# Third layer's weight product as seven half-size products over pairs of tiles, in a fused four-layer graph network

## The reference, cut to what matters

```python
h = jnp.maximum(_layernorm(x, axis=-1), 0.0)
# _L2_gnn_ref: self loops are added to the edges first
norm = dinv[src] * dinv[dst]
h = h @ W                                  # W is 1024 x 1024
out = jax.ops.segment_sum(h[src] * norm[:, None], dst, num_segments=n) + b
x = x + jax.nn.relu(out)
h = jnp.maximum(_layernorm(x, axis=-1), 0.0)   # and the fourth layer: h @ W, attention
```

## Time and profile before

| | |
|---|---|
| time, median of three runs | 986.05 us |
| span of the profiled execution | 985.7 us |
| TensorE busy with matmuls | 968.1 us, 98% |
| VectorE, ScalarE, GpSimd busy | 664.2, 468.8, 138.7 us |
| the third layer's weight product, first matmul to the first of the next layer | 613.70 to 723.40 us |
| in that stage: VectorE, ScalarE busy | 38.5, 12.9 us |

### The profile page before, as it was taken

The page is one execution under the profiler, slowest core; times in us unless marked ns, Lnnn a source line. Parts: engine busy times, 40 slices in busy tenths (PEclk is TensorE's granted clock), DMA queues, the critical chain, the costliest instruction groups (busy, mean ns, idle before and its releaser), DMA issues.

```text
span 985.7 us, 14150 instructions
## 1 busy us (share of the span) xinstructions
PE 968.1 (98%) x5199; PEld 805.6 (82%) x5200; DVE 664.2 (67%) x1193; ACT 468.8 (48%) x719; POOL 138.7 (14%) x191
## 2 busy tenths in 40 slices
PE   4999999999999999999999999999999999999998
PEld 3888878888888888888888888888888888888887
DVE  6987798788788779378884115333346664967777
ACT  5778864554554547223335446001012232766654
POOL 3022400000000001223331000010000000333331
PEclk9999999999999999999999999999999999999999
DMA  6256490000000005543422040733232130201222
GB/s 237 104 191 228 129 268 1 1 23 0 0 21 0 0 0 118 103 147 125 141 93 65 1 172 8 280 118 107 86 128 70 69 122 1 86 20 66 85 85 81
DMA packets 26006, 88.29 MB, mean 90 GB/s; under 512 B 3384, under 2 KB 3580, under 8 KB 25808
## 3 DMA queue, kind: packets, MB, share of 16 engines
q1 hardware_dynamic: 15072, 52.82, 14.8%
q0 software_dynamic: 10880, 34.74, 11.6%
HBM read 59.23 MB, written 33.56 MB: 94 GB/s over the span
## 4 chain that ended last, share of the span: by engine, by line
PE 95%; DVE 1%; ACT 1%; POOL 1%; DMA 1%; issue 0%; SPq 0%; ACTq 0%; DVEq 0%; POOLq 0%
PE ps L615 22%; PE ps L2271 13%; PE ps L2245 11%; PE ps L2165 9%; PE ps L2166 9%; PE ps L2167 9%; PE ps L2221 5%; PE ps L2217 5%; PE ps L598 3%; PE ps L2088 2%; PE ps L2090 1%; PE ps L2089 1%; PE ps L2013 1%; PE ps L2016 1%; PE ps L2057 1%; PE ps L2282 1%
## 5 line engine op out<-in xcount | busy, mean ns | idle before, releaser
L2165 PE MATMUL ps<-g_hi,mask_hi 128*128 128x512 f32 x400 | 157.7, 394 | 0.2 <-DVE mask_lo L1628 0.2
L2167 PE MATMUL ps<-g_hi,mask_lo 128*128 128x512 f32 x400 | 155.9, 390 | 0.0
L2166 PE MATMUL ps<-g_lo,mask_hi 128*128 128x512 f32 x400 | 155.8, 389 | 0.0
L1144 ACT ACTIVATE mask<-ps,v 128x640 f32<-128x640 f32 x80 | 63.2, 793 | 95.7 <-PE ps L2167 49.1
L2271 PE MATMUL ps<-y_all,att_hi 128*128 128x512 f32 x380 | 103.6, 392 | 0.0
L2165 PEld LDWEIGHTS ps<-g_hi,mask_hi 128*128 128x128 f32 x400 | 75.1, 188 | 19.0 <-DVE mask_lo L1628 2.3
L581 ACT ACTIVATE hT_hi<-ps 128x1024 fp32r<-128x1024 f32 x30 | 30.8, 1026 | 123.6 <-PE ps L598 123.4
L2167 PEld LDWEIGHTS ps<-g_hi,mask_lo 128*128 128x128 f32 x400 | 75.1, 188 | 16.0
L2166 PEld LDWEIGHTS ps<-g_lo,mask_hi 128*128 128x128 f32 x400 | 75.1, 188 | 14.8
L615 PE MATMUL ps<-w,hT_hi 128*128 128x512 f32 x320 | 86.6, 392 | 0.0
L2271 PEld LDWEIGHTS ps<-y_all,att_hi 128*128 128x128 f32 x380 | 70.4, 188 | 14.8 <-issue 0.4
(11 more groups left out here) (232 smaller groups left out, 1968.3 us busy)
## 6 DMA issues: line engine op xcount, KB each, us to landing
xin<-x_after SPq DMA_DIRECT2D x20, 512.0 KB, 3.2
xres<-x_after POOLq DMA_DIRECT2D x20, 512.0 KB, 3.6
x_after<-xres POOLq DMA_DIRECT2D x20, 512.0 KB, 2.9
w_raw<-in_L_gnn_W SPq DMA_DIRECT2D x8, 1024.0 KB, 9.8
x_after<-g POOLq DMA_DIRECT2D x20, 256.0 KB, 7.6
xin<-in_x SPq DMA_DIRECT2D x9, 512.0 KB, 3.5
x_after<-in_x SPq DMA_DIRECT2D x8, 512.0 KB, 5.2
weight_rows<-weight_row POOLq DMA_DIRECT2D x8, 512.0 KB, 3.8
```

The lines of the kernel that those rows point to most:

```text
L1144: nc.scalar.activation(mask[k][:, :], U_ALL, ACT.Tanh, bias=v[:, s:s + 1]).then_inc(tanh_ready, 1)
L2165: nc.tensor.matmul(SUMS[dd], mask_hi[k][:, cols], g_hi[:, s, :], start=(s == 0), stop=False)
L2166: nc.tensor.matmul(SUMS[dd], mask_hi[k][:, cols], g_lo[:, s, :], start=False, stop=False)
L2167: last = nc.tensor.matmul(SUMS[dd], mask_lo[k][:, cols], g_hi[:, s, :], start=False, stop=(s == T - 1))
```

## The change

Two tiles of neighbour sums, t and t + 5, are taken as the rows of a 2x2 block matrix (A11, A12 above A21, A22, each 128 rows by 512), the weight as another (B11, B12, B21, B22, each 512 x 512). Their product of eight half-size block products is replaced by one of seven (Winograd's form). For each of the five pairs there are seven **units**, each of 4 blocks by 3 products, 12 matmuls of 128x512 into one bank. The left sides are A11, A12, A22 and four sums S1 to S4 (S1 = A21 + A22, S2 = S1 - A11, S3 = A11 - A21, S4 = A12 - S2), the right sides B11, B21, B22 and four sums T1 to T4. The stream's order is the list `UNITS`.

What this brings with it:

- The factor `dis` of a row is now multiplied in while a pass's banks are read (`take_pass`, one VectorE instruction instead of ScalarE's copy and VectorE's subtraction). For that `dis` is written to DRAM and read back as a row on all partitions.
- VectorE adds and subtracts the blocks S1 to S4 (`add_block`, 20 instructions of 128x512) and the weights' sums (`w2_sum`, 8 of 128x1024).
- Each unit's left side gets its high part from ScalarE (`part_hi_of`) and its low part from VectorE (`part_lo_of`), 35 of each, three units ahead. The seven right sides are split in 14 pieces of 128x1024 on either engine, ten of them during the units (`SPLIT_AT`).
- Each unit's bank is read by one VectorE instruction that adds it to the running sum (`take_unit`, 35 of 128x512). Twenty of these are final halves of a tile; ScalarE takes their positive part (`relu_of`), and GpSimd adds them in DRAM to the layer's input with an accumulating DMA (20 of 256 KB, `add_unit`), in place of ten loads, L1829 and ten stores.
- The third layer's weight is loaded before the passes and not in them; the fourth layer's in two halves behind units 19 and 24. Its eight splits stand at units 25 to 34 (`W3_AT`), the statistics of the fourth layer's first tiles at 28 and 29. The transposes stand in the middle of the last unit.

A unit waits for its left side's low part, its right side's, and for the bank's former user (`unit_read`). The core of the diff:

```diff
+UNITS = ([("A11", t, B11) for t in range(PAIRS)] + [("A12", t, B21) for t in range(PAIRS)] + [("S2", t, T2) for t in range(PAIRS)]
+         + [("S1", t, T1) for t in range(PAIRS)] + [("S4", t, B22) for t in range(PAIRS)]
+         + [unit for n in range(PAIRS + 1) for unit in ([("S3", n, T3)] if n < PAIRS else []) + ([("A22", n - 1, T4)] if n > 0 else [])])
+UNIT_BANKS = (0, 1, 6, 7, 0, 1, 6, 7, 0, 1, 2, 3, 4, 5, 2, 3, 4, 5, 2, 3, 0, 1, 4, 5, 0)
+LATE_BANKS = (1, 2, 3, 0, 1)
+BANK_OF = [LATE_BANKS[t] if kind in ("S3", "A22") else UNIT_BANKS[n] for n, (kind, t, _) in enumerate(UNITS)]
+SPLIT_AT = {0: (T2, 0), 1: (T2, 1), 3: (T1, 0), 4: (T1, 1), 6: (B22, 0), 7: (B22, 1), 11: (T3, 0), 12: (T3, 1), 16: (T4, 0), 17: (T4, 1)}
+W3_AT = {25: 0, 26: 1, 27: 2, 28: 3, 30: 4, 31: 5, 33: 6, 34: 7}
...
+        for n in range(len(UNITS) + 1):
+            if n + BLOCK_LEAD < len(UNITS):
+                part_hi_of(n + BLOCK_LEAD)
+            if n in SPLIT_AT:
+                w2_hi_of(*SPLIT_AT[n])
+            if n - 1 in RELU_UNITS:
+                relu_of(n - 1)
+            if n in W3_AT:
+                split3_act(W3_AT[n])
+            if n in (len(UNITS) - 4, len(UNITS) - 3):
+                h_act(act, dense[2], 0, n - (len(UNITS) - 4))
+            if n == len(UNITS) - 1:
+                transposed_act(act, dense[2], 0, 0)
+                root_act(act, dense[2], 0)
```

```diff
+        for n in range(len(UNITS) + 1):
+            if n + BLOCK_LEAD < len(UNITS):
+                part_lo_of(n + BLOCK_LEAD)
...
+            if n > 0:
+                take_unit(n - 1)
+            if 1 <= n <= PAIRS:
+                add_block("S1", n - 1)
+                add_block("S2", n - 1)
+            if 1 <= n - PAIRS <= PAIRS:
+                add_block("S4", n - PAIRS - 1)
+            if 13 <= n < 13 + PAIRS:
+                add_block("S3", n - 13)
+            if n in SPLIT_AT:
+                w2_lo_of(*SPLIT_AT[n])
+            if n in W3_AT:
+                split_dve(dve, dense[2], [W3_AT[n]])
+            if n in (28, 29):
+                stats_dve(dve, dense[2], 0, n - 28)
+            if n == 29:
+                variance_dve(dve, dense[2], 0)
+            if n == len(UNITS) - 1:
...
+                transposed_dve(dve, dense[2], 0, 0)
...
+        def unit_pe(n):
+            kind, t, w = UNITS[n]
+            pe.wait_ge(part_lo_ready, n + 1)
+            pe.wait_ge(w2_lo_ready, 2 * w + 2)
+            users = [m for m in range(n) if BANK_OF[m] == BANK_OF[n]]
+            if users:
+                pe.wait_ge(unit_read, users[-1] + 1)
...
+            for k in range(QK):
+                if k == QK // 2 and n == len(UNITS) - 1:
+                    transpose_pe(pe, dense[2], 0, 0)
+                for left, rights in ((of[:, 0, k, :], (W2_HI[w], W2_LO[w])), (of[:, 1, k, :], (W2_HI[w],))):
+                    for right in rights:
+                        last = nc.tensor.matmul(UNIT_BANK[n], left, right[:, k, :],
```

More of the change, by code:

```diff
@@ L787, in _ @@
         load_x3(1)
-        sp.wait_ge(w_lo_ready, KT * 4)
-        with sp.Fori(2, HT) as i:
+        sp.wait_ge(w_lo_ready, KT * 3)
+        for i in range(2, HT):
             load_x3(i)
@@ L1248, in _, with relu_of, split3_act @@
+        def relu_of(n):
+            act.wait_ge(unit_read, n + 1)
+            nc.scalar.activation(unit_sum(n), unit_sum(n), ACT.Relu).then_inc(relu_done, 1)
+        def split3_act(k):
+            blocks, adds, pieces = W3_FREE[k]
+            act.wait_ge(part_lo_ready, blocks)
+            act.wait_ge(add_done, adds)
+            act.wait_ge(w2_lo_ready, pieces)
+            split_act(act, dense[2], [k])
         for t in range(T):
@@ L1265, in _ @@
                 root_act(act, d, (t + 2) // 2)
-        last_pass = T * (len(PASSES) - 1)
+        early = {T * FIRST_HALF + n: piece for n, piece in enumerate(((B11, 0), (B11, 1), (B21, 0), (B21, 1)))}
         for n in range(T * len(PASSES)):
@@ L1791, in _ @@
         hs_lo_of(T - 1)
-        d2 = dense[2]
         def low_counts(p):
@@ new lines, in w2_sum, with part_lo_of @@
+        def w2_sum(to, left_of, right_of, op):
+            for j in range(2):
+                some = slice(2 * j, 2 * j + 2)
+                nc.vector.tensor_tensor(to[:, some, :], left_of[:, some, :], right_of[:, some, :], op).then_inc(w2_chain, 1)
+        def part_lo_of(n):
+            kind, t, _ = UNITS[n]
+            of = parts[n % BLOCK_RING]
+            dve.wait_ge(part_hi_ready, n + 1)
+            nc.vector.tensor_tensor(of[:, 1, :, :], sums_block(kind, t), of[:, 0, :, :].bitcast(F32), ALU.subtract).then_inc(part_lo_ready, 1)
@@ L1831, in _ @@
[L1831 to L1845 removed]
+            if p == 0:
+                dve.wait_ge(consts_landed, 48)
@@ L1847, in scores @@
+        scale_dve(dve, dense[2], 0)
+        d3 = dense[2]
         def scores(i, b):
@@ L2251, in _ @@
-        for t in range(T):
-            gcn_product(t)
+        def unit_pe(n):
[5 more added lines that the diff above has]
+                pe.wait_ge(unit_read, users[-1] + 1)
+            elif BANK_OF[n] in (2, 3, 4, 5):
+                pe.wait_ge(sums_read, 2 * len(PASSES))
+            else:
+                pe.wait_ge(sums_read, 2 * len(PASSES) - 2)
+            of = parts[n % BLOCK_RING]
+            for k in range(QK):
[4 more added lines that the diff above has]
+                        last = nc.tensor.matmul(UNIT_BANK[n], left, right[:, k, :],
+                                                start=(kind != "A22" and k == 0 and len(rights) == 2 and right is W2_HI[w]),
+                                                stop=(k == QK - 1 and len(rights) == 1), skip_group_check=True)
+            last.then_inc(unit_done, 1)
@@ L2255, in spread_al @@
+        for n in range(len(UNITS)):
+            unit_pe(n)
         def spread_al(tiles):
```

405 lines of the change are left out of this document (257 added, 148 removed).

## The result

The changed kernel takes 988.88 us, the median of seven runs (986.06 to 991.1), against 986.05 us for the kernel before (also a median of seven). The ratio is 1.0029, with a 95% interval from 1.0018 to 1.0041: slower by 0.3%. The prediction had 985.05 us and "within 0.2%" as the likeliest; its range ended at 988.6, just short of the result.

A forecast was written before the change was run, and what follows sets the result against it. TensorE's matmuls were taken to bound the kernel. The stage going from 109.7 to 107.0 us saves 2.7, a clock fall costs 1.7: 986.05 - 2.7 + 1.7 = 985.05 us, range 982.6 to 988.6.

The forecast's parts named there:

- What the change takes away: In the changed stage 60 matmuls of 0.2267 us fall away, 13.6 us; the new stage takes at least 96.1 us.
- The passes keep their matmuls: In the passes ahead of the stage, the matmuls stay as they were; no cost was put on it.
- The first units: Stage start to unit 11: VectorE's work ends at 27.8 us, before unit 11 starts at 29.9; costed at nothing.
- The room of 2 us: VectorE's spare time up to unit 11's low part, 2.1 us, or 0.055 us per instruction.
- The last ten units: End of stage: VectorE and ScalarE wait for each other, rounds of 4.1 us against 2.72 per unit; 10.9 us of stalls.
- The clock: Behind the 4.9 us stall before the fourth layer's product the clock likelier falls than not; price 0 to 2.3, taken 1.7 us.
- the circle: Late units: ScalarE's weight copy waits behind its positive part, that for VectorE's taking, VectorE's low part for the copy; 4.1 us.
- What was costed at nothing: DMA landings, one-instruction pass reading, weight sums in the fourth pass and GpSimd's additions: 0; a failed landing 0 to 3 us.
- That the clock holds: Rival for the stall before the fourth layer: no clock fall, 983.35 us, between 982.6 and 984.1; chance 0.22.
- That VectorE's instructions are dearer: Rival for the stage: each VectorE instruction 0.06 to 0.18 us more, taken 0.12, giving 990.65 us; chance 0.20.
- That the splits hide: Rival for the last units: no mutual waiting, only a 1.3 us tail from the transposed tile, 973.75 us; chance 0.04.
- That a landing is late: Rival: a DMA behind units 9, 24 or 28 adds 1 to 3 us, giving 986 to 988; chance 0.12.

The follow-up runs named there:

- the filled kernel: Changed kernel with extra matmuls into unread banks ahead of units 31, 33, 34 and behind the last unit, where TensorE would stand: 986.24 us.
- the doubled sums: Changed kernel with 15 more VectorE additions of the same size behind block sums of the first ten units: 993.14 us.
- the kernel with four moves: Changed kernel with weight copies before positive parts, three third-layer weight loads later, transposes with their splits earlier, shifts at units 29 and 32: 973.68 us, stage 97.70.

## Why the prediction was wrong, by its steps

- **What the change takes away**, 13.6 us and a floor of 96.1 for the stage: right. The best kernel comes to 97.70.
- **The step that failed** is "The passes keep their matmuls". They do, 480 of them, but the prediction took from it that they keep their time. It had the loads of the third layer's weight ahead of the passes in its list of what the change brings, where in truth they are issued inside the first one, and gave them no price. It did not ask what of TensorE's stream passes by while they are in flight. There is a branch, and the two together cost 2.7 to 3.2 us in the median: 1.4 to 1.75 of stall, and a clock fall worth 1.8, in two executions of three by the mean clocks of the filled kernel. Without it the kernel takes 985.07 or 985.62 us, by the way it is taken out; the prediction was 985.05.
- **The first units** cost nothing: right. VectorE's low part of unit 11 ends at 641.72 in the changed kernel (its row is at 641.03, 0.69 long), 28.0 us after the stage began, predicted 27.8. The room of 2 us is confirmed by the doubled sums. That VectorE catches up behind unit 12 is right only in the end. It takes unit 17 at 666.75, some 4 us behind that unit's last matmul (613.75 + 18 x 2.72 = 662.7), and TensorE does not wait, as that bank is next written by unit 23. From unit 20 to 24 another round between the two engines stands in the trace, which the prediction had not written down:

```profile
673.26 0.69 DVE L1966 TENSOR_TENSOR parts<-sums,parts 128x512 fp32r<-128x512 f32 x1 [1.22 <-ACT parts L1362]
673.87 0.68 DVE L2007 TENSOR_TENSOR top_right<-ps,second_sum 128x512 f32<-128x512 f32 x1
```

  VectorE waits 1.22 us for the left side's high part, which stands behind the positive part on ScalarE, and the takings at 671.37 and 673.87 are 2.50 us apart, just under a unit's 2.72.
- **The last ten units**: right, in the mechanism (the copy moved by one statement takes 7.7 us out of the stage), in the round (4.08 for 4.1), in the place of each stall and in the length (106.62 for 107.0). The 108.7 us in its paragraph on the profile after is a slip: it adds the clock's 1.7, which by its own account come behind the stage.
- **The clock** behind the stall of 4.5 us: right that it falls, and the size of 1.7 was somewhat low. One execution lost 1.56, another 2.8, outside of the bound of 2.3; the median loses 2.1 to 2.3, by the runs with the stalls filled. So some 0.5 us of the miss are this term's. Right too that a fall in the shorter stalls of the circle costs nothing.
- **What was costed at nothing**: the landings of DMAs, the weights' sums and GpSimd's additions cost nothing, as said. But GpSimd's additions do not all fall where VectorE is ahead: from 663 to 671 us they stretch the instructions of a VectorE that is behind (see the end).
- **The rivals.** That the clock holds gave 983.35; a kernel in which it does, and without the branch, took 983.28. That VectorE's instructions are dearer is refuted: 0.68 to 0.69 each in the first units and the last ten; the few at 1.18 to 1.20 stand beside GpSimd's additions. That the splits hide gave 973.75; the kernel with four moves takes 973.68, but by moves that this rival did not have, so the likeness proves nothing for it. That a landing is late is refuted too: no VectorE, ScalarE or GpSimd instruction of the stage waits for a DMA. The result lies just above the range (988.88 against 988.6), for a reason that none of the cases had.
- **The sum for the typical run**: 985.8 - 3.1 (stage) + 2.2 (clock at its end) + 3.0 (branch) + 0.2 (time outside of the span) = 988.1; measured 988.3 to 988.9. The terms for the clock and the branch are differences of the very runs that the sum explains, so only the remainder, 0.2 to 0.8 us, tests it.

The gain of the change is then accounted for: of 13.6 us the order of two statements on ScalarE took 7.7 (106.62 - 98.87), the late preparation of the next layer's tile 1.2 (98.87 - 97.70), 1.6 are left over the floor of 96.1, and the clock, the branch and the time outside of the span took 5.4. Together 15.9, which is 2.3 more than the gain.

What stays open: why this branch of TensorE waits while the DMA engines are full, and the one 2.6 us before it does not. The trace shows one instruction packet, on a DMA queue of its own, between 539 and 543 us. It may be that the loads hold it up, but it starts at 539.4, ahead of the stall (540.56 to 541.98), and one starts at 540.2 in the run with the branch later, where nothing stands; no run parts this from other ways in which a full DMA could hold the branch.

## What to carry to other kernels

When two engines work in turn inside a short unit, write down the whole round across both streams. VectorE and ScalarE were 79% and 48% busy in this stage and still ran its last ten units at 4.08 us a round instead of 2.72, and one statement's place on the less busy engine was worth 1%. Ask of every moved DMA not only when it lands, but what else goes on while it is in flight; in this kernel that was control flow on the bounding engine. And count also a short stall of TensorE, such as the 1.68 us here, with what its clock costs behind it, unless another wait follows soon that takes it up.

## What the runs showed of the hardware that was not expected

- The granted clock fell behind stalls of 1.68 us and of 2.60 us, not only behind those of 4 us and more, and the length alone does not settle it. Behind the stall of 4.5 us it fell in all six profiles that have one; behind that of 2.6 to 2.8 us at unit 31 in three of six; behind that of 1.42 to 1.75 us at the branch in one of six, at 1.68 and not at 1.75. Where it fell, matmuls ran at the 1.2 GHz level for some 3 us (542.90 to 546 in the passes) to 6 us (719.22 to 725 behind the stage); the cost was 1.5 to 2.8 us where no later wait took it up. The same program loses it in one execution and not in another, and that makes its times scatter: 985.9 to 991.1 for the changed kernel, 982.5 to 984.8 for the same kernel with the stalls filled and the branch free.
- The branch of TensorE in the second pass takes no time that shows while the DMA engines are idle (share 0.02), and 1.42 to 1.75 us with their share at 1.05 and 400 GB/s. The one in the first pass shows no wait at a share of 0.86 to 1.03.
- GpSimd's additions of the bias (L1011, 1.7 us each, the first 3.4) and VectorE's instructions stretch each other. Their timelines after:

```profile
660.02 5.12 POOL L1011 TENSOR_TENSOR second_sum<-second_sum,row_all 128x512 f32<-128x512 f32 x2 [10.86 <-DVE second_sum L2007]
```

```profile
660.45 1.22 DVE L1952 TENSOR_TENSOR w_lo<-b,w_hi 128x1024 fp32r<-128x1024 f32 x1
661.58 0.68 DVE L1966 TENSOR_TENSOR parts<-sums,parts 128x512 fp32r<-128x512 f32 x1
...
662.79 1.20 DVE L1984 TENSOR_TENSOR sums<-sums 128x512 f32<-128x512 f32 x1
663.90 2.32 DVE L1952 TENSOR_TENSOR w_lo<-b,w_hi 128x1024 fp32r<-128x1024 f32 x1
...
666.75 0.68 DVE L2007 TENSOR_TENSOR second_sum<-ps,first_sum 128x512 f32<-128x512 f32 x1
```

  The rows of 662.79 and 663.90 take 1.20 for 0.68 and 2.32 for 1.22. Those of 660.45 and 661.58 keep their times, and it is GpSimd's first addition that takes 3.4 us beside them. Instructions that read one operand from PSUM keep their 0.68 (662.19, 669.65). It cost nothing here, though VectorE was behind: it took unit 17, at 666.75, some 4 us late, and TensorE did not stand. The Trainium skill, page "SBUF — State Buffer", section "Who interferes with whom", says that a VectorE instruction with two inputs in SBUF contends with a GpSimd instruction that reads SBUF, and that one with at most one such input does not, outside of its two-port modes. The rows agree.
